# State-space scans: one GpSimd product per state for all four channel blocks, in place of two

## The reference, cut to what matters

```python
def _mamba(x, in_w, conv_w, conv_b, xproj_w, dt_w, dt_b, A_log, D_param, out_w):
    xh, z = jnp.split(x @ in_w.T, 2, axis=-1)
    xc = jax.nn.silu(conv_b + sum((xp[:, k:k + L, :] * conv_w[:, k] for k in range(D_CONV))))
    proj = xc @ xproj_w.T                        # dt, Bm (16 states), Cm (16 states)
    delta = jax.nn.softplus(dt @ dt_w.T + dt_b)
    deltaA = jnp.exp(jnp.einsum('bld,dn->bldn', delta, A))
    deltaBu = jnp.einsum('bld,bln->bldn', delta * xc, Bm)
    def step(h, inp):
        dA, dBu, c = inp
        h = dA * h + dBu
        return (h, jnp.einsum('bdn,bn->bd', h, c))
    y = ys + xc * D_param
    return (y * jax.nn.silu(z)) @ out_w.T
```

## Time and profile before

| what | value |
|---|---|
| median of 3 runs | 5131.06 us (5128.0 to 5135.81) |
| the profiled execution: span from its first to its last instruction | 5202.0 us |
| PE busy in the whole span | 4518.9 us, 87% |
| DVE busy | 3442.4 us, 66% |
| ACT busy | 2164.4 us, 42% |
| POOL busy | 2384.8 us, 46% |
| granted TensorE clock, mean | 0.930 |
| input products, line 1691 | 512 operations, 2107 ns each |
| output products, line 1702 | 256 operations, 2106 ns each |
| scans, line 1755 | 1024 operations, 1104 and 1077 ns each |

### The profile page before, as it was taken

One profiled execution on the slowest core, in us unless ns is written; L12 is line 12 of the kernel. 1 busy time (PEld: TensorE's weight loads), 2 busy tenths in 40 slices (PEclk: granted clock), 3 DMA queues, 4 the chain that ended last, 5 costly groups with the idle time before them and its releaser, 6 DMA issues. The chain is left out here.

```text
span 5202.0 us, 64516 instructions
## 1 busy us (share of the span) xinstructions
PE 4518.9 (87%) x22312; PEld 2888.0 (56%) x22312; DVE 3442.4 (66%) x7100; ACT 2164.4 (42%) x4039; POOL 2384.8 (46%) x1510
## 2 busy tenths in 40 slices
PE   7888599858888888888887899797899899999999
PEld 4555267633333333333332455596444799999998
DVE  3764222258898998988988323211886788888885
ACT  3654011125555555555555223232664233333332
POOL 3442400169999999999999000000122123222332
PEclk8998799979999999999998899898999899999999
DMA  2003113322222222222222000374000200000000
GB/s 72 1 1 113 60 60 116 120 72 69 69 69 72 69 69 69 69 71 70 69 69 65 17 1 7 123 267 155 1 0 1 87 3 5 5 5 5 5 5 5
DMA packets 153108, 287.18 MB, mean 55 GB/s; under 512 B 24441, under 2 KB 135024, under 8 KB 144206
## 3 DMA queue, kind: packets, MB, share of 16 engines
q1 hardware_dynamic: 144926, 263.59, 15.5%
q0 software_dynamic: 6656, 14.04, 0.9%
q10 hardware_dynamic: 1200, 5.42, 0.3%
HBM read 252.33 MB, written 33.42 MB: 55 GB/s over the span
## 5 line engine op out<-in xcount | busy, mean ns | idle before, releaser
L1509 PE MATMUL ssm_ps<-ssm_hc,net_ident 128*128 128x452 f32 x2048 | 961.5, 596 | 191.6 <-DVE ssm_hc L1765 105.9
L1691 POOL TENSOR_TENSOR ssm_dBu<-ssm_du,ssm_bc 128x904 f32<-128x904 f32 x512 | 1066.5, 2107 | 3.2 <-POOL ssm_du L1709 1.7
L1610 ACT ACTIVATE ssm_ps<-ssm_step,ssm_decay 128x448 f32<-128x448 f32 x1024 | 647.5, 636 | 646.9 <-DVE ssm_ps L1755 435.4
L1509 PEld LDWEIGHTS ssm_ps<-ssm_hc,net_ident 128*128 128x128 f32 x2048 | 392.5, 204 | 727.7 <-issue 347.1
L1755 DVE TENSOR_TENSOR_SCAN ssm_ps<-ssm_ps,ssm_dBu 128x452 f32<-128x452 f32 x512 | 565.0, 1104 | 131.6 <-ACT ssm_ps L1610 45.2
L1755 DVE TENSOR_TENSOR_SCAN ssm_hs<-ssm_ps,ssm_dBu 128x452 f32<-128x452 f32 x512 | 551.2, 1077 | 41.5 <-ACT ssm_ps L1610 35.0
L1702 POOL TENSOR_TENSOR ssm_hc<-ssm_hs,ssm_bc 128x904 f32<-128x904 f32 x256 | 539.2, 2106 | 74.2 <-DVE ssm_hs L1755 74.1
L3135 POOL TENSOR_TENSOR peer_hid<-peer_hid,peer_weight 128x452 f32<-128x452 f32 x256 | 294.1, 1188 | 525.0 <-ACT peer_weight L3082 525.0
L2993 PE MATMUL peer_ps<-peer_xn,peer_down 128*128 128x226 f32 x2048 | 439.3, 361 | 0.0
L3061 PE MATMUL peer_ps<-peer_hid,peer_up 128*128 128x226 f32 x2048 | 400.7, 354 | 3.1 <-POOL peer_hid L3135 2.2
L3061 PEld LDWEIGHTS peer_ps<-peer_hid,peer_up 128*128 128x128 f32 x2048 | 386.4, 189 | 12.9 <-POOL peer_hid L3135 6.2
(11 more groups left out here) (424 smaller groups left out, 7871.0 us busy)
## 6 DMA issues: line engine op xcount, KB each, us to landing
ssm_bc<-ssm_rows SPq DMA_DIRECT2D x256, 452.0 KB, 3.6
ex_w<-in_l_ffn_w SPq DMA_DIRECT2D x64, 1024.0 KB, 6.6
moe_w_gu<-in_moe_gate_up SPq DMA_DIRECT2D x16, 704.0 KB
slots_in<-rt_zeros SPq DMA_DIRECT2D x17, 640.0 KB, 8.7
moe_rows_in<-slots_in SPq DMA_DIRECT2D x16, 512.0 KB
slots_out<-xp_rows_out SPq DMA_DIRECT2D x16, 512.0 KB
moe_w_dn<-in_moe_down SPq DMA_DIRECT2D x16, 384.0 KB
peer_down<-in_peer_down_t SPq DMA_DIRECT2D x1, 4096.0 KB, 16.6
```

The lines of the kernel that those rows point to most:

```text
L1509: nc.tensor.matmul(Y_BANK[j][:, 0:GT], c["ident"][:, :], hc[:, q % 2, j, :], start=False, stop=(n == S - 1))\
L1610: nc.scalar.activation(rows(dA(i % 2))[:, :, lo:lo + N - 1], rows(step[hf.d][:, j, :])[:, :, lo:lo + N - 1], ACT.Exp, scale=decay[hf.d][:, ...
L1691: nc.gpsimd.tensor_tensor(dBu[:, q % 2, j:j + 2, :], du[hf.d][:, j:j + 2, :], bc[:, q % RING, 0:1, :].to_broadcast([P, 2, GT]), ALU.mult). ...
```

## The change

`input_terms` makes the products of all four blocks in one operation of 128 x 1808. It waits until all four scans of state q - 2 are done (before, its first operation waited for three of them and its second for all four), and, for state 0 of a half, for both operations of `step_input`. The scans of a state wait for that one operation. At n = 15 the single operation for the next half's state 0 stands behind du(2).

```diff
-                    def input_terms(hf, n, j):
+                    def input_terms(hf, n):
 
                         q = S * hf.r + n
                         pool.wait_ge(landed[q % RING], 16 * (q // RING + 1))
                         if q >= 2:
-                            pool.wait_ge(s["scan_done"], IB * (q - 2) + AT[j + 1] + 1)
+                            pool.wait_ge(s["scan_done"], IB * (q - 1))
                         if q == 0:
                             pool.wait_ge(mixed_done, B)
                         if n == 0 and hf.fronts:
-                            pool.wait_ge(s["du_done"], 2 * (hf.fronts - 1) + j // 2 + 1)
-                        nc.gpsimd.tensor_tensor(dBu[:, q % 2, j:j + 2, :], du[hf.d][:, j:j + 2, :],
-                                                bc[:, q % RING, 0:1, :].to_broadcast([P, 2, GT]), ALU.mult).then_inc(s["dbu_done"], 1)
+                            pool.wait_ge(s["du_done"], 2 * hf.fronts)
+                        nc.gpsimd.tensor_tensor(dBu[:, q % 2, :, :], du[hf.d][:, :, :],
+                                                bc[:, q % RING, 0:1, :].to_broadcast([P, IB, GT]), ALU.mult).then_inc(s["dbu_done"], 1)
...
                             if hf.rec and n + 1 < S:
-                                input_terms(hf, n + 1, 0)
-                                input_terms(hf, n + 1, 2)
+                                input_terms(hf, n + 1)
                             if n == S - 3 and hf.front:
                                 step_input(hf, 0)
                             if n == S - 1:
-                                if hf.after:
-                                    input_terms(halves[k + 1], 0, 0)
                                 if hf.front:
                                     step_input(hf, 2)
                                 if hf.after:
-                                    input_terms(halves[k + 1], 0, 2)
+                                    input_terms(halves[k + 1], 0)
...
-                        dve.wait_ge(s["dbu_done"], 2 * q + j // 2 + 1)
+                        dve.wait_ge(s["dbu_done"], q + 1)
```

## The result

The changed kernel takes 5186.5 us in the median (5180.3 to 5191.1, 4 runs) against 5131.2 before (5128.0 to 5135.8, 4 runs): ratio 1.0107, 95% interval 1.0094 to 1.012, 55 us slower. Forecast were 5181 and a range of 5157 to 5205.

A forecast was written before the change was run, and what follows sets the result against it. VectorE was taken to set the pace of states 0 to 10, GpSimd of 11 to 15. About +3.5 us in each of 15 halves (+52), -0.8 in the last and 1 off gave +50: 5181 us, range 5157 to 5205.

The forecast's parts named there:

- What bounds the kernel: State-space stage: VectorE sets the pace of states 0 to 10, GpSimd that of the light states 11 to 15.
- Part 1, the product: On GpSimd, one operation in place of two takes 3.97 us against 4.15 for the pair: 0.18 us saved.
- Part 2, the wait for four blocks in the middle: States 0 to 10: scans waiting for all four blocks cost nothing, with a thin cover of at least 0.4 us.
- rival (c): Large product slower per element, or the thin cover in states 1 to 4 breaks: slower still, 5207 us; 8%.
- Part 3, the seam: Between two halves: state 0's whole product stands behind du(2) and VectorE stands still some 5 us; +3.6 us per seam.
- Rival (d): At the seam: du(2) waits for something later than slot 62, costing 2 us in place of 3.6; 5157 us; 7%.
- Part 4, the end of a half: I(15) is needed whole: 29.5 us from state 11 to du(2), against 29.3 before; +0.2 us.
- The last half: No front, GpSimd never waits: +1.9 us at its seam, less 15 x 0.18, is -0.8.
- The sum: Whole stage: about +3.5 us for each of 15 halves, +52; last half -0.8; 1 off for small waits: +50 us.
- rival (b): VectorE's seam stall is partly paid back in early states, product near 3.76 us: within 0.2%, 5131 to 5139 us; 6%.

The follow-up runs named there:

- the middle split again: Changed kernel with two products again in states 1 to 10 of each half, each scan there waiting for its own pair: 5250.1 us, ratio 1.0107 to the kernel before.
- the first experiment: Changed kernel, but state 0's blocks 0 and 1 made ahead of du(2), 2 and 3 behind, scans waiting for own pair: 5212.1 us, ratio 1.0030 to kernel before.
- the sixth: Changed kernel, but two products in states 0, 1 and 15, state 0's first pair ahead of du(2): 5197.9 us, ratio 1.0003 to the kernel before.
- The order alone: Kernel before, two products per state, but the next state 0's first product moved behind du(2): 5212.9 us, ratio 1.0034.
- the wait alone: Kernel before, two products per state in the old order, but every scan waits for both: 5237.1 us, ratio 1.0078.

## Why the prediction was right

Point by point, by its own parts:

- *What bounds the kernel.* Right, and tested: with the middle split again the time did not move, so VectorE does set the pace of states 1 to 10, and the wait of O(10) wipes out what GpSimd gains there. Two readings were slightly off. From the second scan of state 0 to the first of state 11 there are 10.75 states, not 10.5, so VectorE's pace was 6.8 us and not 7.0. And the earlier wait that the text puts at O(7) is that of O(8): 1.8 us before, 2.8 after.
- *Part 1, the product.* Forecast 3.97 us and a saving of 0.18; measured 4.01 and 0.14. The middle of the 3.94 and 4.04 us of that part is 3.99, not 3.97, which would have been nearer. The slope from 904 to 1808 elements is (4.009 - 2.107) / 904 = 2.10 ns per element, inside the 2.03 to 2.14 of the earlier trace rows and nearer its upper end.
- *Part 2, the wait for four blocks in the middle.* It costs nothing there, as said. In the half shown, the products of states 1 to 4 end 0.4 to 0.7 us before the first scans of these states, so the cover, thin as it is, held. With the product under 4.21 us as well, rival (c) did not come true. But the cover existed only because the seam had already made VectorE late. With the seam repaired the same wait cost 1.35 us in state 1, in the first experiment, and 1.16 us in state 2, in the sixth. The fourth scan of state q - 2 does make GpSimd wait, in one state: 0.97 us behind the taps of slot 38, which the text had put at nothing. It is hidden by the wait that follows.
- *Part 3, the seam.* Forecast +3.60, measured 8.03 - 4.39 = +3.64, and within 0.3 us of that at every seam but the first, where it was 2.9. Rival (d) is out with it: du(2) waited for slot 62, as forecast.
- *Part 4, the end of a half.* Forecast 29.5, measured 29.7, because of the 0.04 us that the product is longer, four times over.
- *The last half.* Forecast -0.8; this is the term that was wrong in sign. From du(2), the scan of block 1 of the last state starts 2844.76 - 2745.03 = 99.7 us later, before 2857.64 - 2759.74 = 97.9: +1.8. Two things explain it. The saving per product was 0.14 and not 0.18, 0.6 us over 15 products, and at the very end the scans of state 15 have to wait for the whole of I(15), so the last output product waits 1.9 us for them. The text said that GpSimd never waits in this half and had no term for it. -0.8 + 0.6 + 1.9 gives +1.7.
- *The sum.* The text took off 1 us for small waits that the stall would hide; the middle stretches show 4.4 us less, all that there is of the paying back of rival (b). The ends of the halves show 3.3 us more, where the sum had next to nothing. That these two misses nearly cancel is luck. And the steps of +3.8 and +3.4 for the two halves have a mean of 3.6, or 54 us, where the text went on with 3.5 and 52; 3.50 a half was measured.

The terms come to 52.5 + 1.8 = 54 us of the 55 measured; the rest is within the noise.

The order alone cost 16 us and the wait alone 40, and the shorter product, at five places of 15 halves, is worth 5 x 0.14 x 15 = 10 us. That makes 46, not 55. The missing part is what the order alone gave back at du(2), 13.4 us in all. With the wait for all four blocks in place it gives nothing back, since du(2) then waits for its step size in any case: the trace of the wait alone shows 0.94 us of it behind Ia, in every half. So the sum is 16 + 13 + 40 - 10 = 59, near the 55 measured. The marks say the same without the medians. From the wait alone to the changed kernel the seam grows by 1.88 us a half, near the 2.05 of Ia less the 0.14 of the shorter product, and the end of a half shrinks by 0.55, which is four times 0.14 and leaves nothing for the order.

## What to carry to other kernels

When two engines take turns, a saving on one counts only in the stretches in which that engine has no wait, so find these in the timeline before adding it up. Of the 16 shortened products of a half, only the one at the seam and the four at the end lay on the path here. And an operation that is merged takes the later of its two start conditions and the later of its two ends: look first at the place in the list where the parts stood on two sides of a wait (here du(2)), because the first part was filling that wait. Merge by place, not everywhere.

## What was not expected

- The kernel before, unchanged, ran at 5131 us in two sessions and at 5197 in two others (those at 5197 were on chips 1 and 7, the second at 5131 on chip 6). The offset of 65 us lies ahead of the stage. The changed kernel itself was timed only in the two sessions at 5131, with ratios of 1.0107 and 1.0106; with its middle split again it had 1.0107 in one at 5197. What causes the offset was not tried.
- Putting a product ahead of a wait can delay what waits: in the kernel before, Ia held du(2) up by 0.8 us or so, and with Ia behind it half of the cost of the order came back. Whether the best order is a third one (both products of state 0 behind du(2), and the step sizes earlier) was not tried.
